# A post-norm decoder layer on one core: magnitudes of the second factor on VectorE, half tiles in every batch

## The reference, cut to what matters

```python
def act_quant(x):
    scale = 127.0 / jnp.clip(jnp.max(jnp.abs(x), axis=-1, keepdims=True), EPS)
    q = jnp.clip(jnp.round(x * scale), -128.0, 127.0) / scale
    return x + jax.lax.stop_gradient(q - x)

def h_bitlinear(x, w):
    xq = act_quant(fwht(x))          # Walsh-Hadamard transform along the row, then int8 per token
    wq = weight_quant(w)             # ternary
    return jnp.einsum('bsh,oh->bso', xq, wq)

gate = h_bitlinear(hidden_states, w_gate)     # 512 -> 2048
up = h_bitlinear(hidden_states, w_up)
return h_bitlinear(jax.nn.silu(gate) * up, w_down)   # 2048 -> 512
```

## Time and profile before

| | us |
|---|---|
| median of 3 runs | 1088.88 |
| the profiled execution | 1086.8 |
| its span, first to last instruction | 1084.9 |
| TensorE busy | 936.8 (86%) |
| VectorE busy | 875.3 (81%) |
| ScalarE busy | 678.9 (63%) |
| GpSimd busy | 231.3 (21%) |

### The profile page before, as it was taken

How to read it: one execution, slowest core, us unless ns; L and a number is a source line. 1 busy time by engine, 2 the same in 40 slices (tenths; PEclk the granted TensorE clock), 3 DMA queues, 4 the chain that set the end, 5 groups by cost and what they waited for, 6 DMA issues and landing times. The chain is left out here.

```text
span 1084.9 us, 13454 instructions
## 1 busy us (share of the span) xinstructions
PE 936.8 (86%) x4128; PEld 358.6 (33%) x4128; DVE 875.3 (81%) x1670; ACT 678.9 (63%) x1115; POOL 231.3 (21%) x248
## 2 busy tenths in 40 slices
PE   3567699999999999999898879897989889889966
PEld 1223233322222222222222444353444334343422
DVE  7997688899999999999897589658755776578467
ACT  3787688888888889877666234354524553275351
POOL 4203411122222331232201422140005000320001
PEclk9688899999999999999999999999999999999988
DMA  8956765566666556664442323120233004100501
GB/s 328 383 179 238 222 177 162 178 190 197 190 196 192 162 175 196 197 184 144 132 123 91 116 70 75 41 104 1 60 96 117 1 7 139 48 2 3 172 20 39
DMA packets 90684, 145.00 MB, mean 134 GB/s; under 512 B 12339, under 2 KB 52147, under 8 KB 89078
## 3 DMA queue, kind: packets, MB, share of 16 engines
q1 hardware_dynamic: 90614, 144.16, 42.3%
HBM read 84.75 MB, written 42.21 MB: 117 GB/s over the span
## 5 line engine op out<-in xcount | busy, mean ns | idle before, releaser
L402 DVE TENSOR_REDUCE neg_max<-banks 128x1 f32<-128x512 f32 x512 | 327.7, 682 | 32.8 <-PE banks L374 29.2
L1396 ACT ACTIVATE probs<-banks 128x512 f32<-128x512 f32 x512 | 277.1, 606 | 76.7 <-PE banks L1299 75.8
L1313 PE MATMUL banks<-probs,v_st 128*32 128x512 f32 x1024 | 137.9, 612 | 0.6 <-ACT probs L1396 0.6
L1850 PE MATMUL banks<-q_T,f_int_all 128*128 128x512 bf16 x512 | 122.9, 379 | 14.1 <-DVE h_ring L1871 10.1
L374 PE MATMUL banks<-attn_T,x_T 96*128 96x512 bf16 x256 | 98.6, 393 | 19.6 <-DVE neg_max L402 13.6
L1195 POOL TENSOR_TENSOR rstd<-vare,half 128x1 f32<-128x1 f32 x48 | 29.2, 608 | 401.1 <-DVE vare L1187 401.1
L1865 ACT ACTIVATE h_ring<-h_ring 128x512 f32<-128x512 f32 x64 | 40.3, 630 | 106.1 <-DVE h_ring L1860 106.1
L374 PE MATMUL banks<-k_st,q_st 96*128 96x512 bf16 x256 | 98.3, 384 | 7.8 <-DVE neg_max L402 6.4
L1299 PE MATMUL banks<-q_st,k_st 99*128 99x512 bf16 x256 | 96.0, 383 | 3.8 <-ACT probs L1396 1.8
L1299 PE MATMUL banks<-x_T,attn_T 99*128 99x512 bf16 x256 | 97.9, 382 | 0.1
L409 POOL TENSOR_TENSOR rest<-y,parts 128x512 f32<-128x512 f32 x32 | 37.6, 1174 | 211.7 <-ACT parts L382 211.6
(11 more groups left out here) (286 smaller groups left out, 1555.1 us busy)
## 6 DMA issues: line engine op xcount, KB each, us to landing
f_int_all<-in_ffn_dram SPq DMA_DIRECT2D x24, 512.0 KB, 7.6
qk_parts<-parts SPq DMA_DIRECT2D x32, 384.0 KB, 2.6
woT<-in_ffn_dram SPq DMA_DIRECT2D x24, 512.0 KB, 6.5
qk_parts<-parts SPq DMA_DIRECT2D x32, 256.0 KB, 2.9
pv_rows<-pv_z SPq DMA_DIRECT2D x32, 256.0 KB, 5.5
hz<-h_turned SPq DMA_DIRECT2D x32, 256.0 KB
x_T<-qk_parts SPq DMA_DIRECT2D x16, 384.0 KB, 3.9
attn_T<-qk_parts SPq DMA_DIRECT2D x16, 384.0 KB, 4.9
```

Source lines behind the costliest of these rows:

```text
L402: dve.tensor_reduce(neg_max[:, g.h, tile:tile + 1], s_bank[(16 * g.n + tile) % SB], AX.X, ALU.max, negate=True).then_inc(max_done, 1)
L1313: last = pe.matmul(pv_bank[32 * j:32 * j + 32, :], v_st[g.v][:, kt].rearrange("p h d -> p (h d)")[:, (HD + 1) * head:(HD + 1) * head + 2 * ...
L1396: act.activation(probs[ktp][:, j, i, :], st_bank[(16 * g.n + 2 * w + i) % STB], ACT.Exp).then_inc(exp_done, 2)
L1850: last = pe.matmul(bank, f_int[w][:, k * FF + ch.start:k * FF + ch.stop], q1_T[:, k, :], start=k == 0, stop=k == KD - 1)
```

## The change

ScalarE no longer writes absolute values. VectorE reads each copied pair from `hz` and reduces it over the two blocks with `apply_absolute_value`, into `h_max` for the first pair and into `h_abs` for the others, which one more maximum folds into `h_max`. TensorE's waits for a bank are moved from the absolute value to the copy.

Scaling and rounding is done in half tiles in all batches. VectorE rounds tiles 0 and 2, ScalarE 1 and 3, except in the last batch, where it is 0 and 1 by VectorE, 2 and 3 by ScalarE. `HALF_AT` and `ACT_HALF_AT` say in which iteration each half (tile, part) is done.

In the last batch the four down tiles use four banks. The read of the last down bank of batch b - 1, which stood ahead of the read of the context product xm(0), stands behind it.

```diff
@@ dve_xm
-            if n == 0:
-                need(dve, "d_read", 4 * (B - 1))
+            if B >= 2:
+                need(dve, "d_read", 4 * (B - 2) + n + 1)
@@ down_bank
-                return psum[6 + t % 2] if b >= NB - 2 else LOW
+                return psum[t] if b == NB - 1 else psum[6 + t % 2] if b == NB - 2 else LOW
@@ pe_gate_up, pe_h2
-                            need(pe, "h_abs", 8 * b)
+                            need(pe, "h2_sb", 8 * b)
-                    need(pe, "h_abs", 8 * b + p - 1)
+                    need(pe, "h2_sb", 8 * b + p - 1)
@@ act_h2
                 did(act.copy(hz[:, 2 * p:2 * p + 2, :], pair_banks(p)), "h2_sb")
-                need(act, "maxed", 16 * b + 2 * p - 2)
-                need(act, "bias_o_ready", 2)
-                did(act.activation(magnitudes(p), pair_banks(p), ACT.Abs), "h_abs")
@@ dve_max
-                need(dve, "h_abs", 8 * b + p + 1)
-                for a in range(2):
-                    ...
-                        did(dve.tensor_tensor(h_max[:], magnitudes(p)[:, a, :], h_max[:], ALU.max), "maxed")
+                need(dve, "h2_sb", 8 * b + p + 1)
+                if p == 0:
+                    need(dve, "top_mm", b)
+                out = h_abs[:, p % 2, :] if p else h_max[:]
+                did(dve.tensor_reduce(out, hz[:, 2 * p:2 * p + 2, :].rearrange("p a s -> p s a"), AX.X, ALU.max,
+                                      apply_absolute_value=True), "h_part")
+                if p:
+                    need(dve, "h_part", 8 * b + p + 1)
+                    need(dve, "maxed", 7 * b + p - 1)
+                    did(dve.tensor_tensor(h_max[:], out, h_max[:], ALU.max), "maxed")
@@ tables
+            HALF_AT = {2: ((0, 0),), 3: ((0, 1), (1, 0)), 4: ((1, 1),), 5: ((2, 0),), 6: ((2, 1), (3, 0)), 7: ((3, 1),)}
+            ACT_HALF_AT = {4: (1, 0), 5: (1, 1), 7: (3, 0), 8: (3, 1)}
@@ dve_first
-                    if b and 2 <= i < 6:
-                        dve_scale2(dve, b - 1, i - 2)
-                    if b and i in (3, 5):
-                        dve_q2(dve, b - 1, i - 3)
-                    if b and down_end(b, i - 1) is not None:
+                    for t, part in HALF_AT.get(i, ()) if b else ():
+                        dve_half_scale(dve, b - 1, t, part)
+                        if t in dve_tiles(b - 1):
+                            dve_half_q2(dve, b - 1, t, part)
+                    if b and i < FK - 1 and down_end(b, i - 1) is not None:
                         dve_final(dve, b - 1, down_end(b, i - 1))
@@ dve_second
                 dve_xm_norm(dve, B, 0)
+                if b:
+                    dve_final(dve, b - 1, KD - 1)
                 dve_xm(dve, B, 1, FRONT)
+                if b:
+                    dve_final_norm(dve, b - 1, KD - 1)
```

More of the change, by code:

```diff
@@ L1894, in sp_shuffle @@
                 need(sp, "y_sb", g + 1)
-                need(sp, "q2_ready", 2 * b)
-                need(sp, "q2_dve", 2 * b)
+                need(sp, "q2_ready", 4 * b)
+                need(sp, "q2_dve", 4 * b)
                 at = spread_row(i)
@@ L1968, in act_mul, with dve_tiles, act_tiles, half_of @@
                 did(act.copy(mul_row[:], MUL_BANK), "mul_sb")
-            def dve_scale2(dve, b, t):
-                tile = hz[:, :, token_tile(t)]
+            def dve_tiles(b):
+                return (0, 1) if b == NB - 1 else (0, 2)
+            def act_tiles(b):
+                return (2, 3) if b == NB - 1 else (1, 3)
+            def half_of(a, t, part):
+                return a[:, 8 * part:8 * part + 8, token_tile(t)]
+            def half_made(b, t, part):
+                at = 4 * b + part + 1
+                if t in dve_tiles(b):
+                    return "q2_dve", at + 2 * dve_tiles(b).index(t)
+                return "q2_ready", at + 2 * act_tiles(b).index(t)
@@ L1972, in dve_scale2, with dve_half_scale @@
+            def dve_half_scale(dve, b, t, part):
                 need(dve, "mul_sb", b + 1)
                 need(dve, "h2_sb", 8 * b + 8)
[L1974 to L1994, removed]
-                did(dve.tensor_scalar(q2_T[:, :, token_tile(t)], hz[:, :, token_tile(t)], MAGIC, -MAGIC, ALU.add,
-                                      ALU.add), "q2_dve")
@@ L1998, in half_of @@
-            def half_of(a, t, part):
-                return a[:, 8 * part:8 * part + 8, token_tile(t)]
-            def half_made(t, part):
-                at = 2 * (NB - 1) + part + 1
-                return ("q2_ready", at) if t == ACT_TILE else ("q2_dve", at + 2 * DVE_TILES.index(t))
-            def dve_half_scale(dve, t, part):
-                need(dve, "mul_sb", NB)
-                need(dve, "h2_sb", 8 * NB)
                 tile = half_of(hz, t, part)
@@ L2031, in pe_down @@
                 if part == 0:
-                    if b < NB - 1:
-                        need(pe, ("q2_dve", "q2_ready")[t % 2], 2 * b + t // 2 + 1)
-                    if b >= NB - 2:
+                    if b == NB - 1:
+                        need(pe, "h2_sb", 8 * NB)
+                    elif b == NB - 2:
                         if t < 2:
@@ L2042, in pe_down @@
                         need(pe, "row1_sb", b + 2)
-                if b == NB - 1:
-                    need(pe, *half_made(t, part))
+                need(pe, *half_made(b, t, part))
                 for k in range(8 * part, 8 * part + 8):
@@ L2216, in dve_first @@
                 dve_h(dve, b, FK - 1)
-                if b and b < NB - 1:
-                    dve_final_norm(dve, b - 1, KD - 1)
             def pool_first(pool, b):
@@ L2370, in _ @@
                     act_mul(act, b)
-                    for part in range(2):
-                        act_half_round(act, ACT_TILE, part)
-                        act_half_q2(act, ACT_TILE, part)
+                    for t in act_tiles(b):
+                        for part in range(2):
+                            act_half_round(act, b, t, part)
+                            act_half_q2(act, b, t, part)
                 @block.gpsimd
@@ L2425, in _ @@
                         for part in range(2):
-                            dve_half_scale(dve, t, part)
-                            if t != ACT_TILE:
-                                dve_half_q2(dve, t, part)
+                            dve_half_scale(dve, b, t, part)
+                            if t in dve_tiles(b):
+                                dve_half_q2(dve, b, t, part)
                     for t in range(KD):
```

40 lines of the change are left out of this document (15 added, 25 removed).

## The result

| | before | after |
|---|---|---|
| median of 5 runs each, one chip | 1089.87 us (1086.02 to 1090.83) | 1071.48 us (1066.14 to 1072.48) |
| the profiled execution | 1086.8 us | 1066.14 us |
| ratio after/before | | 0.9838, 95% interval 0.9817 to 0.9860 |

What follows compares the result with a forecast made beforehand. No engine bounds the kernel everywhere: ScalarE's order decides between the loops, TensorE mostly in them. Terms +9.9 - 3.4 - 6.6 - 2.9 + 1.1 = -1.9 us gave 1087 for the median, range 1068 to 1103.

Steps and rivals of the forecast that it cites:

- rival 1: VectorE's magnitude reads run at full rate, 1.22 us a pair: sum -19.9 us, to 1069; chance 0.17.
- the forecast case: Whole kernel: the terms sum to -1.9 us, 1087 for the median, own range 1082 to 1092; chance 0.38.
- The price R: VectorE's reduction of one copied pair, 1024 elements in: 1.9 us taken, range 1.22 to 3.4.
- The stretches: Between the gate/up loops, three times: the magnitudes on VectorE delay each by 3.3 us, +9.9 in all.
- The two loops: Loops of batches 1 and 2: half tiles gain 1.7 us each, reading xm(0) before the final 3.3 each.
- the fourth final: Batches 1 and 2's loops: final(3) behind the read of xm(0) saves 1.8 us plus 1.5 of slow matmuls, each.
- Batch 3's loop: Half tiles remove a wait of 1.96 us and a slow stretch of 0.93: -2.9, bounds -1.5 and -3.7.
- The last batch: Behind the shuffles: pairs every 2.65 us instead of 2.0 cost +4.3, the end gains -3.2; together +1.1.
- The tail: Last batch behind the mul row: four banks end the wait for bank 6, final(3) 3.2 us earlier.
- rival 2: Magnitudes ahead of the tops' transpose are dearer, above 2.13 us each: slower than before, 1106 at 2.5; chance 0.22.
- Rival 4: Magnitude price right, slow stretches go wholly, 3 to 4 us of delay between the loops hides: 1082; chance 0.14.
- Rival 3: Other waits take 6 of the 12.9 us gained by the half tiles and the moved final: 1093; chance 0.09.

Runs made afterwards that it cites:

- m1: The changed kernel with reductions of other forms added on VectorE behind its last store; 1024 elements took 1.22 to 1.24 or 1.87 to 1.89 us by form.
- e2: The changed kernel with whole tiles scaled and rounded in the loops, as before, the last batch as changed; 1069.28 us, 0.9815 of before.
- e3: The changed kernel with the fourth final of batches 0 and 1 back ahead of the read of xm(0); 1075.16 us, 0.9868 of before.
- e5: The kernel before with only the magnitudes moved to VectorE, finals, halves and banks as before; 1075.98 us, 0.9868 of before.
- e7: The changed kernel with batch 2's last half rounded by VectorE in iteration 7, not ScalarE in 8; 1066.45 us (0.9769 of before), again 1066.42 us (0.9790).
- e4: The changed kernel with two alternating down banks in the last batch, ScalarE still doing tiles 2 and 3; 1068.57 us, 0.9796 of before.
- e9: The changed kernel with four down banks, but in the last batch ScalarE rounds only tile 2 and VectorE the others; 1071.01 us in one run.

## Why the prediction came out as it did

The time fell into the range, but by rival 1 (chance 0.17) and not by the forecast case: 18 us where -1.9 was forecast and -19.9 was rival 1's. That rival 1 met the sum to 2 us is in part luck, since two of its terms were off the other way: batch 3's loop gave 3.6 less than it said, and the two loops and the last batch 2.3 more.

- **The price R: the step that failed.** 1.9 was taken, 1.22 to 1.25 was measured in all 32. The reasoning from two reductions with equal excess per element was right for their kind (m1: 1.87 to 1.89 for 1024 elements), but both had 4 or 7 inputs a result, and the trace of before had no reduction of two distant inputs. "The nearest row" was near in step and not in inputs. The rule of the Trainium skill ("SBUF — State Buffer", the note on cachelines in the section "Door 1: The DMA port swizzle") that each change of line pays is not borne out by this read: its pattern steps 2 KB at every element, and it took 1.23 us for 1024, as dense passes do. In m1 a price does show with four or more inputs apart.
- **The stretches.** Forecast +3.3 each, rival 1 said -0.9; measured -0.6, -0.8, -1.0. The forecast's order was right: the wait behind w1(2) came, 1.75 for 1.9. With each magnitude 0.67 longer, less the 0.94 that VectorE waits ahead of pair 4's magnitude, the last maximum would by my estimate have stood 4.4 later than it did, which is 3.4 behind its place before: the forecast's +3.3. So the order and the waits were right, and R was mis-sized. The gain at full clock is 1.8; the slow part ahead of the tops takes 0.8 to 1.2 of it.
- **The two loops.** Forecast -5.0 each, measured -5.8, of other parts. That the sum is near is in part luck. The rows it named came: wait at the first down half gone, 2.41 ahead of down(1) for 2.7, 1.21 and 3.67 at xm(1) for 1.2 and 3.6. But the halves themselves are worth 0.9 (e2) and the fourth final 1.8 (e3), not 1.7 and 3.3; the other 3.1 were slow stretches, which vanish when the magnitudes alone are moved (e5). The forecast tied each slow stretch to the wait ahead of it; waits of 2.30 and 3.02 stand in these traces with and without one.
- **Batch 3's loop: a second step that failed.** Forecast -2.9, "the loop is TensorE's, so it is kept"; measured +0.7. TensorE's down work did end 3.2 earlier (55.32 behind the tops for 58.48). It was given back to a wait of 3.66 for the last shuffle. The prediction noted that the shuffles would issue 2 to 3 later (it was 2.5) and let two iterations of slack cover it; that slack ends where TensorE gets faster and the queue does not. e7 gets 2.7 of it back against the repeat of the changed kernel (1.8 in its first profile). The forecast's two pieces, the wait of 1.96 and the slow 0.93, can't both be put down to the half tiles either: in e5 the slow matmuls are gone with whole tiles.
- **The last batch.** Pairs came every 1.87 to rival 1's 1.9, -1.7 for the -1.1 said. The tail was forecast -3.2 and measured -3.4, with four banks as the reason; e4 and e9 show that the tile split alone does it as well.
- **Rivals 2 to 4.** R is under 2.13, so rival 2 fell with the forecast. Rival 4 took R as priced and fell with it too. Rival 3's mechanism, a gain eaten by another wait, happened in batch 3's loop for 3.6 us.

## What to carry to other kernels

When a price is taken from the nearest row, list every way in which that row differs from the new operation (here the inputs per result); an axis on which all the known rows agree is one that they say nothing about. When two engines' work is shortened in a loop, follow the DMA chain that the loop also feeds, since slack counted in iterations shrinks with them. And test parts both alone and left out: two edits may each recover the same wait, and then neither is missed when removed.

## What the runs showed of the hardware

- VectorE reduces 1024 fp32 elements in 1.22 to 1.24 us with two inputs a result, 16 bytes, 128 bytes or 2 KB apart (up to 1.25 in the kernel itself), or with adjacent inputs, 2 or 8 of them (m1); with 4 or 8 inputs apart at 128 bytes or 2 KB, and with 16 at 2 KB, it takes 1.87 to 1.89.
- TensorE's granted clock falls to about 0.5 (its 1.2 GHz level) for some 3 us behind some idle stretches and not behind others of the same length and neighbourhood: 2.30 us of idle was followed by eight matmuls in 2.57 (before), 2.63 (e2, first loop), 1.90 (e2, second loop) and 1.90 (e5); 3.02 by 5.11 (before), 6.72 (e3, first loop), 3.67 (e3, second loop) and 3.67 (e5). What decides it these runs don't show.
